# A hybrid layer on one core: one opening block with a quarter of x, and the causal attention's constants made beside the first FFN's choice

## The chip, the cores and the metric

The kernel runs on one core of one Trainium2 chip. The metric is the device time of one execution in microseconds (us), the median of several executions. A core has TensorE (PE), VectorE (DVE), ScalarE (ACT), GpSimd (POOL) and SyncE (SP). They run their own instruction streams and meet only at semaphores. In this kernel SP and ACT issue the DMAs. The kernel is a sequence of blocks; a block ends when every engine has come to its end, and the next one starts then.

## The reference, cut to what matters

x is 8 x 1024 tokens of 256 values, float32. Four sublayers are added to it one after the other, each on a layer norm of x:

```
x = x + attn_a(layernorm(x))     # 16 heads of 16; a query sees the keys at 40 offsets back (0..32, 48, 64, ... 384),
                                 # scores + pos_bias[offset, head], softmax; times sigmoid(x @ Wgate + bgate), @ Wout + bout
x = x + ffn(layernorm(x))        # 32 experts, each takes its 8 best tokens of a batch, merged by weight;
                                 # one row per expert through w1, gelu, w2; scattered back by weight
x = x + attn_b(layernorm(x))     # causal attention, 16 heads of 16, W1/b1 (q, k, v interleaved by head), W2/b2
x = x + ffn(layernorm(x))        # the same experts again
```

layernorm has no scale or shift: (x - mean) / sqrt(var + 1e-5).

## The kernel before

**The whole.** x stays in SBUF for the whole kernel as `x_sb`, 64 tiles of 128 tokens. The stages are: `build_constants` (L83), `band_attention` (L250), `ffn` "f1_" (L1480), `dense_attention` (L1007), `ffn` "f2_". Every sublayer leaves `bn_stats` of its new x in `stats`; the next one aggregates them to mean and variance (`bn_aggr`), ACT takes a square root (L364, L1104, L1537), DVE a reciprocal (L123), and `z` is the normalised x (L733, L1364, L1679).

**The opening.** `build_constants` is a block of its own: SP loads x in four quarters (L93), DVE runs `bn_stats` on each as it lands (L101), POOL builds the identity. Then comes the setup block of band attention (L317 to L407). SP loads weights and bias rows (L323 to L333), waits for DVE's `row_steps` and moves the split bias rows (L335). ACT loads the position biases (L351), waits until DVE has spread them over four short lines (L374 to L382), sends the lines to DRAM, each repeated for every row of a block (L355), waits until they have landed, and loads them back as sliding windows, `bias_k` and `bias_q`, with 12 DMAs (L362); then it takes the square root, and waits for the windows. DVE does the lines, a permutation, the normalizers of all 64 tiles (L393), the scaling of the q weights and the split of the bias rows into three bf16 parts (L403 to L406). In the block after it DVE first fills the ones rows of seven key stacks, three PSUM slots and `outT_ps` (L714 to L718), and POOL clears the value tiles (L464 to L466); PE and ACT wait for all of that (`cleared`).

**Band attention** follows a hand-written list of steps, `band_schedule()` (L149): each engine walks the same list and does its part of each step, so a step's place in the list is its place in every engine's and queue's order. A batch's heads come in four groups g of four. The steps: `z`, `zt` (PE transposes z, ACT copies), `q`/`k` (PE projects, DVE adds the bias), then its division into three bf16 parts for exactness (`part0` ACT, `rest1` POOL, `part1` ACT, `part2` POOL, each part stored to DRAM by ACT, the last as `store2`), `stack` (SP loads the parts back as stacked operands for two heads), `turn` (ACT and POOL reorder the stack for the far offsets, L870 and L502), `v`/`vout`/`vin` (values through DRAM), `mx` (PE scores for the row maxima, DVE reduces, L780), `fparts`, `fp`, `mred`, `mt`, `mrow` (the maxima of four heads become three bf16 rows under the queries' stack, by SP's DMAs L528), `S` (PE scores minus the maxima, DVE adds the position bias, L771, ACT exponentiates, L833), `PV`, `ote`, `ot`, `at`, `op`. PSUM gives three slots of two banks, used in turn by the steps that need one; a step waits until the slot's user three before it has been read. Projections of the next batch are put between the steps of this one (`fillers`, `between`), and the division of a q or k is spread over the steps behind it (L231 to L238). The first batch has no earlier one, so the list starts with its own opening (L204 to L207):

```
first = [("z", 0, 0), ("zt", 0, 0), ("z", 0, 1), ("zt", 0, 1)] + projection("q", 0, 0) + projection("k", 0, 0)
first += operands(0) + operands(1) + operands(2) + operands(3) + turned(0) + turned(1) + turned(2) + projection("q", 0, 1) + projection("k", 0, 1)
first += [step for i4 in range(2) for step in (("v", 0, i4), ("vout", 0, i4))]
first += [("mx", 0, 0, h) for h in range(HG)] + [("fparts", 0, 0), ("fp", 0, 0), ("mred", 0, 0), ("mt", 0, 0), ("mrow", 0, 0)]
```

**Causal attention** (`dense_schedule`, L915) is built in the same way, with SP storing and loading (`spill`, L1178, `stack`, L1190, `mrow`, L1195). `maxima(b, g)` gives 18 `mx` steps, then `mred`, `mt` and `mrow`; a stack holds four heads. The parts of q and k of a batch's first half (`projections(b, 0)`) feed stacks g = 0 and 1, those of the second half g = 2 and 3. Its list starts with L979 to L981:

```
seq = tokens(0) + projections(0, 0) + [("stack", 0, 0)] + projections(0, 1) + [("stack", 0, 1)] + values(0)
for steps in maxima(0, 0):
    seq += steps
```

Its setup block (L1068 to L1119) loads the weights with 13 DMAs of short runs on SP, builds a bf16 identity and the causal mask on POOL, and computes the normalizers and the parts of the bias rows on DVE. In the next block DVE fills the ones rows of three key stacks (L1350), `outT_ps` and `neg_off` before its first z.

**The FFN** has a setup block (L1521: normalizers, small loads, and the first 8 MB of expert weights into rings), a block that chooses the tokens (L1580: no work for SP and POOL in it; at its end DVE copies the merged tokens, L1739), and a block that runs the experts and adds the result to x (L1772).

## Time and profile before

| | |
|---|---|
| median of 3 runs | 3498.59 us (3488.94, 3498.59, 3508.78) |
| profiled execution | 3486.47 us, of which the span from first to last instruction is 3484.7 us |
| PE busy | 2844.4 us, 82% of the span |
| DVE busy | 1644.5 us, 47% |
| ACT busy | 1435.7 us, 41% |
| POOL busy | 794.2 us, 23% |
| mean granted TensorE clock | 0.914 of full speed |
| first matmul | 91.36 us |
| first instruction of f1_, of causal attention's setup | 1440.2 us, 1713.5 us |

Busy time is the time with an instruction of that engine in flight; the rest is waiting. "DVE ... [6.70 <-POOL b_parts L1217]" in a row of the timeline says that DVE was idle for 6.70 us before this instruction and that the last thing it waited for was POOL's instruction of line 1217 on `b_parts`. SPq and ACTq are the DMA issues of SP and ACT; their duration is that of issuing, not of the transfer. In the windows view the columns are the stretch, its length, the busy time (and instruction count) of PE, PE's weight loads, DVE, ACT and POOL, the granted TensorE clock, the share of the DMA engines and the GB/s that they moved.

### The profile page before, as it was taken

What the parts mean: (1) busy time and instruction counts of PE and PEld (TensorE: products, weight loads), DVE (VectorE), ACT (ScalarE), POOL (GpSimd) and SP (SyncE); (2) the same over time, 40 slices, a digit from 0 to 9 for tenths busy, and PEclk for the clock granted to TensorE, in tenths of its full rate; (3) what the DMA queues carried; (4) which work ended last, traced back from release to release, by engine and by line L of the source; (5) the groups of instructions that cost most, each with busy time, mean ns of one, the idle gap of its engine ahead of it and who ended that gap; (6) DMA issues with size and microseconds to landing.
All of it is one profiled execution on the core that took longest, in us unless ns stands there. A gap on an engine that the chain in (4) does not pass through costs nothing. (4 is left out here: it accounts for less than half of the span.)

```text
span 3484.7 us, 101224 instructions
## 1 busy us (share of the span) xinstructions
PE 2844.4 (82%) x45724; PEld 1622.0 (47%) x45724; DVE 1644.5 (47%) x2755; ACT 1435.7 (41%) x1422; POOL 794.2 (23%) x555
## 2 busy tenths in 40 slices
PE   0487888888888887689468989898989998997897
PEld 0255565655555555434234444444444444443443
DVE  5134434344344344520546666666665666664401
ACT  0245444444444453330115555454545454554401
POOL 0324343333434242000222112121211121210002
PEclk9778888889898989799669999999999999999998
DMA  5324233333324341259232212222222222220397
GB/s 142 86 57 113 73 84 79 92 88 78 94 63 106 78 99 48 106 230 403 62 91 50 61 43 60 46 57 50 59 49 56 55 56 56 56 47 35 158 422 265
DMA packets 233547, 344.23 MB, mean 99 GB/s; under 512 B 113690, under 2 KB 142180, under 8 KB 216740
## 3 DMA queue, kind: packets, MB, share of 16 engines
q1 hardware_dynamic: 207892, 310.02, 30.5%
q10 hardware_dynamic: 25232, 27.83, 3.5%
q8 instruction: 357, 5.85, 0.7%
q14 instruction: 66, 0.54, 0.1%
HBM read 266.15 MB, written 69.24 MB: 96 GB/s over the span
## 5 line engine op out<-in xcount | busy, mean ns | idle before, releaser
L1403 DVE TENSOR_REDUCE b_tops<-b_slot 128x8 f32<-128x1024 f32 x576 | 680.4, 1220 | 360.6 <-PE b_slot L1260 181.5
L1440 ACT ACTIVATE b_probs<-b_slot 128x1024 f32<-128x1024 f32 x576 | 582.5, 1022 | 549.6 <-PE b_slot L1260 393.2
L502 POOL COPY a_q_far<-a_q_near 96x1024 bf16<-96x1024 bf16 x128 | 259.1, 2054 | 344.9 <-PE a_slot L581 218.5
L1207 POOL TENSOR_SCALAR_AFFINE_SELECT b_probs<-b_probs 128x1024 f32<-128x1024 f32 x128 | 139.6, 1091 | 809.1 <-ACT b_probs L1440 809.1
L1280 PE MATMUL b_outT_ps<-b_probs,b_v 128*17 128x128 f32 (+3 forms) x4608 | 317.6, 383 | 6.2 <-ACT b_probs L1440 5.5
L1260 PE MATMUL b_slot<-b_q_stack,b_k_stack 99*128 99x512 bf16 (+3 forms) x1280 | 273.1, 320 | 43.8 <-DVE b_tops L1403 32.8
L870 ACT ACTIVATE a_k_far<-a_k_near 96x1024 bf16<-96x1024 bf16 x128 | 258.3, 2068 | 86.6 <-DMA a_k_near<-parts_near_dram 78.1
L1260 PE MATMUL b_slot<-b_k_stack,b_q_stack 96*128 96x512 bf16 (+3 forms) x1280 | 265.7, 322 | 29.5 <-DVE b_tops L1403 20.8
L771 DVE TENSOR_TENSOR a_probs<-a_slot,a_bias_k 128x1024 f32<-128x1024 f32 x128 | 154.6, 1218 | 192.4 <-PE a_slot L581 192.3
L780 DVE TENSOR_REDUCE a_tops<-a_slot 128x16 f32<-128x1024 f32 x128 | 156.3, 1222 | 118.1 <-PE a_slot L581 117.1
L833 ACT ACTIVATE a_probs<-a_probs 128x1024 f32<-128x1024 f32 x128 | 133.1, 1052 | 183.7 <-DVE a_probs L771 164.6
L1260 PEld LDWEIGHTS b_slot<-b_q_stack,b_k_stack 99*128 99x128 bf16 x1280 | 106.4, 99 | 203.7 <-DVE b_tops L1403 61.9
L1876 PE MATMUL f_ps<-f_w_ring,f_hidT 128*32 128x256 f32 x1024 | 184.0, 381 | 2.1 <-ACT f_hidT L1924 2.1
L1260 PEld LDWEIGHTS b_slot<-b_k_stack,b_q_stack 96*128 96x128 bf16 x1280 | 97.4, 98 | 185.0 <-DVE b_tops L1403 61.4
L621 PE MATMUL a_slot<-a_bias_q,a_ident 128*128 128x512 bf16 x256 | 102.3, 491 | 84.8 <-POOL a_q_far L502 27.0
L657 PE MATMUL a_outT_ps<-a_probs,a_v_near 128*17 128x64 f32 (+1 forms) x8448 | 152.8, 227 | 19.2 <-issue 15.3
L657 PEld LDWEIGHTS a_outT_ps<-a_probs,a_v_near 128*17 128x17 f32 x8448 | 127.9, 102 | 85.8 <-issue 76.8
L1855 PE MATMUL f_ps<-f_w_ring,f_lhs 128*32 128x512 f32 x512 | 146.7, 606 | 8.0 <-POOL f_lhs L1834 8.0
L1956 DVE TENSOR_TENSOR f_pre<-f_ps,f_b1T 128x128 f32<-128x128 f32 x32 | 7.8, 286 | 299.8 <-PE f_ps L1864 299.8
L1280 PEld LDWEIGHTS b_outT_ps<-b_probs,b_v 128*17 128x17 f32 x4608 | 96.3, 96 | 112.5 <-issue 68.1
L589 PE MATMUL a_slot<-a_zT,a_wqk 128*128 128x512 f32 x256 | 144.2, 670 | 3.9 <-issue 2.7
L799 DVE TENSOR_SCALAR a_zb<-a_slot,a_bqk 128x1024 f32<-128x1024 f32 x32 | 41.1, 1284 | 220.9 <-PE a_slot L589 180.6
(220 smaller groups left out, 4334.1 us busy)
## 6 DMA issues: line engine op xcount, KB each, us to landing
f_w_ring<-in_L_ffn_w_dram SPq DMA_DIRECT2D x128, 1024.0 KB, 9.1
parts_near_dram<-a_parts ACTq DMA_DIRECT2D x96, 256.0 KB
parts_dram<-b_parts SPq DMA_DIRECT2D x96, 256.0 KB
a_k_near<-parts_near_dram SPq DMA_DIRECT2D x128, 128.0 KB, 3.0
b_k_stack<-parts_dram SPq DMA_DIRECT2D x64, 256.0 KB, 6.9
a_q_near<-parts_near_dram SPq DMA_DIRECT2D x64, 192.0 KB, 2.9
b_q_stack<-parts_dram SPq DMA_DIRECT2D x32, 384.0 KB, 4.4
values_dram<-a_v_stage SPq DMA_DIRECT2D x16, 544.0 KB, 4.4
```

The source lines that it names most:

```text
L502: pool.tensor_copy(q_far[far][0:QK_ROWS, h, :].rearrange("p (r a) -> p r a", r=LINKS), q_near[near][0:QK_ROWS, h, :].rearrange("p (a r) -> ...
L589: return pe.matmul(dst[:, c * 512:(c + 1) * 512], wqk[:, "qk".index(kind), kd, 8 * part:8 * part + 8, :].rearrange("p h d -> p (h d)"), zT ...
L657: ins = pe.matmul(outT_ps[BLK * h:BLK * h + HD + 1, lo:top], v_near[:, c, blk % 4, (HD + 1) * h:(HD + 1) * (h + 1)], probs[h][:, at:at + t ...
L771: ins = dve.tensor_tensor(probs[h][:, :].rearrange("p (k t c) -> p k t c", k=2, c=64), src[:, :].rearrange("p (k t c) -> p k t c", k=2, c=64),
L780: ins = dve.tensor_reduce(tops[:, h, :, :].rearrange("p k t -> p (k t)"), src[:, :].rearrange("p (t c) -> p t c", c=64), AX.X, ALU.max)
L870: act.activation(k_far[far][0:QK_ROWS, h, :].rearrange("p (r a) -> p r a", r=LINKS), k_near[near][0:QK_ROWS, h, :].rearrange("p (a r) -> p ...
L1260: ins = pe.matmul(dst[:, at:at + top - lo], own[0:rows, head, P * tile:P * tile + P], other[0:rows, head, lo:top], start=True, stop=True)
L1280: ins = pe.matmul(outT_ps[32 * h:32 * h + HD + 1, first:last], v1[b % 2][:, j, HG * g + h, :], src[:, base + first:base + last], start=u = ...
L1403: ins = dve.tensor_reduce(out, src, AX.X, ALU.max)
L1440: act.activation(probs_of(b, g, u, h)[:, :], slot_of(step)[:, :], ACT.Exp).then_inc(taken_act, 1)
L1855: ins = pe.matmul(bank[n][32 * j:32 * j + 32, :], lhs1[half][:, kd, j, :], w1_ring[:, j, kd, n * 512:(n + 1) * 512], start=kd == 0, stop=k ...
L1876: ins = pe.matmul(bank[4 + half][32 * j:32 * j + 32, 0:D], hidT[half][:, c, j, :], w2_ring[:, j, c, :], start=c == 0, stop=c == HE // P - 1)
```

## The change

1. `build_constants` is gone. Its work is in band attention's setup block: SP issues one quarter of x first and the other three behind weights and rows; DVE runs `bn_stats` and the normalizers for this quarter (batches 0 and 1) alone; POOL builds both identities.
2. In that block POOL also does the memsets of the value tiles and of the seven key stacks' ones rows, and DVE those of the PSUM tiles. The semaphore `cleared` is gone. The windows (`bias_in`) are waited for by PE's first `mx` and DVE's first `S`, no longer by ACT at the block's end; ACT takes its square root behind the issue of the windows, as before.
3. The statistics of the other quarters are steps `x_stats` of the band's list (groups 0, 2 and 3 of batch 0), their normalizers the steps `norms` and `rstd` in group 0 of batch 1, with a square root on ACT.
4. Band attention's opening is reordered: v and the maxima of the first group come before the second half's q projection, whose k projection goes into the first group.
5. Causal attention's constants are allocated around the FFN and loaded and built in the FFN's choice block (SP, POOL, two scalings on DVE). Its setup block is gone; DVE computes the normalizers at the head of its main block. The memsets of the first stack, `outT_ps` and `neg_off` come behind the second z, those of the other two stacks ahead of DVE's copy of the first k.
6. Causal attention's opening is reordered: v first, then the second half's q and k between the first group's maxima, and stack (0, 1) behind them.

The diff, cut to its core:

```diff
-def build_constants(nc, ident, x, x_sb, stats):
...
 # band_schedule
             if not earlier:
-                return [], [], [("gate", b, 0)], [], [], [("gate", b, 1)]
+                return [], [("k", 0, 1)], [("gate", b, 0)], [("x_stats", 1, 0), ("x_stats", 1, 1)], [("x_stats", 1, 2), ("x_stats", 1, 3)], \
+                    [("gate", b, 1)]
...
-    first += operands(0) + operands(1) + operands(2) + operands(3) + turned(0) + turned(1) + turned(2) + projection("q", 0, 1) + projection("k", 0, 1)
+    first += operands(0) + operands(1) + operands(2) + operands(3) + turned(0) + turned(1)
     first += [step for i4 in range(2) for step in (("v", 0, i4), ("vout", 0, i4))]
-    first += [("mx", 0, 0, h) for h in range(HG)] + [("fparts", 0, 0), ("fp", 0, 0), ("mred", 0, 0), ("mt", 0, 0), ("mrow", 0, 0)]
+    first += [("mx", 0, 0, h) for h in range(HG)] + turned(2) + [("fparts", 0, 0)] + projection("q", 0, 1)
+    first += [("fp", 0, 0), ("mred", 0, 0), ("mt", 0, 0), ("mrow", 0, 0)]
...
+            if b == 0 and g in (2, 3):
+                place[3].extend([("x_stats", g, 0), ("x_stats", g, 1)])
+                place[4].extend([("x_stats", g, 2), ("x_stats", g, 3)])
+            if (b, g) == (1, 0):
+                place[4].append(("norms",))
+                place[5].append(("rstd",))
...
 # band_attention, setup block, SP
+                    quarter(0)
...
+                    for n in range(1, B // 2):
+                        quarter(n)
                     sp.wait_ge(row_steps, 6)
                     sp.dma_start(bias_rows[:, :, :], row_parts[0:1, :, :, :]).then_inc(rows_in, 16)
                     sp.wait_ge(weights_in, 16 * n_loads)
                     sp.wait_ge(rows_in, 64)
...
 # POOL
+                    pool.memset(v_near[:, :, :, :], 0.0)
+                    pool.memset(v_far[:, :, :], 0.0)
+                    pool.memset(v_stage[:, :, :, :], 1.0).then_inc(ident_made, 1)
+                    pool.wait_ge(ident_made, 5)
+                    for stack in k_near + k_far:
+                        pool.memset(stack[QK_ROWS:ALL_ROWS, :, :], 1.0)
...
 # ACT, behind the 12 DMAs of the windows
-                    act.wait_ge(stat_steps, STATS_STEPS)
-                    act.activation(std[:, :], std[:, :], ACT.Sqrt).then_inc(std_ready, 1)
-                    act.wait_ge(bias_in, 16 * 12)
+                    act.wait_ge(norm_steps, 2 * NT + 1)
+                    act.activation(std[:, 0:2 * NT], std[:, 0:2 * NT], ACT.Sqrt).then_inc(std_ready, 1)
...
 # DVE
+                    for slot in slots:
+                        dve.memset(slot[:, :], 0.0)
+                    dve.memset(outT_ps[:, :], 0.0)
...
-                    layer_norm_stats(dve, std_ready, stat_steps, stats, mv, std, rstd)
+                    dve.wait_ge(x_loaded[0], 16)
+                    for t in range(2 * NT):
+                        ins = dve.bn_stats(stats[:, t, :], x_sb[:, t, :])
+                    ins.then_inc(line_steps, 1)
+                    dve.wait_ge(line_steps, n_lines + 7)
+                    normalizers(dve, 0, 2 * NT, 0)
...
+                    dve.wait_ge(std_ready, 1)
+                    dve.reciprocal(rstd[:, 0:2 * NT], std[:, 0:2 * NT])
...
 # band_attention, main block, DVE
-                for stack in k_near + k_far:
-                    dve.memset(stack[QK_ROWS:ALL_ROWS, :, :], 1.0).then_inc(cleared, 1)
-                for slot in slots:
-                    dve.memset(slot[:, :], 0.0).then_inc(cleared, 1)
-                dve.memset(outT_ps[:, :], 0.0).then_inc(cleared, 1)
...
+                    elif kind == "x_stats":
+                        _, n, k = step
+                        dve.wait_ge(x_loaded[n], 16)
+                        for t in range(2 * n * NT + 4 * k, 2 * n * NT + 4 * k + 4):
+                            ins = dve.bn_stats(stats[:, t, :], x_sb[:, t, :])
...
 # dense_schedule
-    seq = tokens(0) + projections(0, 0) + [("stack", 0, 0)] + projections(0, 1) + [("stack", 0, 1)] + values(0)
-    for steps in maxima(0, 0):
-        seq += steps
+    seq = tokens(0) + projections(0, 0) + [("stack", 0, 0)] + values(0)
+    first, second = [step for steps in maxima(0, 0) for step in steps], projections(0, 1)
+    seq += first[:6] + second[:6] + first[6:12] + second[6:] + [("stack", 0, 1)] + first[12:]
...
 # dense_attention: the setup block (loads, identity, mask, parts of the bias rows, normalizers) is removed; main block, DVE
-                for n in range(DEPTH):
-                    dve.memset(k_stack[n][QK_ROWS:ALL_ROWS, :, :], 1.0).then_inc(cleared, 1)
-                dve.memset(outT_ps[:, :], 0.0).then_inc(cleared, 1)
-                dve.memset(neg_off[:, :, :], -LOWEST).then_inc(cleared, 1)
-                dve.wait_ge(cleared, N_CLEARED)
+                layer_norm_stats(dve, std_ready, stat_steps, stats, mv, std, rstd)
+                dve.wait_ge(stat_steps, STATS_STEPS + 1)
...
+                        if (b, i4) == (0, 1):
+                            dve.memset(k_stack[0][QK_ROWS:ALL_ROWS, :, :], 1.0).then_inc(cleared, 1)
+                            dve.memset(outT_ps[:, :], 0.0).then_inc(cleared, 1)
+                            dve.memset(neg_off[:, :, :], -LOWEST).then_inc(cleared, 1)
...
+                            if (kind, b, half) == ("k", 0, 0):
+                                for stack in k_stack[1:]:
+                                    dve.memset(stack[QK_ROWS:ALL_ROWS, :, :], 1.0).then_inc(cleared, 1)
...
 # ffn, choice block: SP issues the 13 loads (the two rows first) and the bias rows, POOL makes
 # identity, mask and the three parts of the rows (3 copies, 2 subtractions), DVE:
+                    if beside:
+                        dve.wait_ge(weights_in, 16 * n_loads)
+                        dve.tensor_scalar(dense["bqk"][:, 0, :], dense["bqk"][:, 0, :], HD ** -0.5, None, ALU.mult)
+                        dve.tensor_scalar(dense["wqk"][:, 0, :, :, :], dense["wqk"][:, 0, :, :, :], HD ** -0.5, None, ALU.mult)
                     dve.wait_ge(merge_done, B * NT)
...
 # build
-        build_constants(nc, ident, a["L0_attn_a_x"], x_sb, stats)
-        band_attention(nc, x_sb, stats, ident, attn_a, scratch)
-        ffn(nc, x_sb, stats, ident, experts, scratch, "f1_")
-        dense_attention(nc, x_sb, stats, ident, attn_b, scratch)
+        band_attention(nc, a["L0_attn_a_x"], x_sb, stats, ident, attn_a, scratch)
+        with ExitStack() as dense:
+            constants = dense_constants(nc, dense)
+            ffn(nc, x_sb, stats, ident, experts, scratch, "f1_", beside=(constants, attn_b))
+            dense_attention(nc, x_sb, stats, ident, constants, scratch)
```

## Rows read from the trace of the kernel before

**Rows 1.** Stretches (windows view): length, busy us of each engine, granted clock, DMA share, GB/s.

```profile
0.00:27.00 27.00, 0.00 (x0) 0.00 (x0) 15.97 (x48) 0.00 (x0) 0.70 (x6) 1.00 0.98 311
...
33.40:53.70 20.30, 0.00 (x0) 0.00 (x0) 8.64 (x123) 0.00 (x0) 0.60 (x3) 1.00 0.63 119
53.70:64.00 10.30, 0.00 (x0) 0.00 (x0) 0.92 (x4) 1.54 (x2) 0.00 (x0) 1.00 1.12 152
...
300.00:1400.00 1100.00, 918.90 (x27986) 636.23 (x27974) 463.76 (x632) 496.46 (x385) 388.14 (x244) 0.88 0.33 83
```

**Rows 2.** Timeline, setup: start us, length, engine, line, operation, out<-in, count [idle before].

```profile
0.82 14.46 SPq L93 DMA_DIRECT2D x_sb<-in_L_attn_a_x_dram  x4
...
9.19 5.32 DVE L101 BATCH_NORM_STATS2 stats<-x_sb 128x6 f32<-128x256 f32 x16 [9.19 <-DMA x_sb<-in_L_attn_a_x_dram]
...
33.38 0.41 ACTq L351 DMA_DIRECT2D a_pos<-n_L_attn_a_pos_bias_dram  x1
...
39.48 0.70 ACTq L355 DMA_DIRECT2D line_k_dram<-a_line_k  x1
...
53.69 1.94 ACTq L362 DMA_DIRECT2D a_bias_k<-line_k_dram  x4
...
62.79 0.26 ACT L364 ACTIVATE a_std<-a_std 128x64 f32<-128x64 f32 x1
...
67.90 0.85 SPq L335 DMA_DIRECT2D a_row_home<-a_row_parts  x1
70.35 1.91 POOL L464 MEMSET a_v_near<- 128x2176 f32 x1 [36.21 <-POOLq L317]
...
89.83 1.38 DVE L733 TENSOR_SCALAR a_zb<-x_sb,a_mv,a_rstd 128x256 f32<-128x256 f32 x4
```

**Rows 3.** Timeline, band attention, from its first projections to its first S.

```profile
97.86 16.30 PE L589 MATMUL a_slot<-a_zT,a_wqk 128*128 128x512 f32 x32 [1.11 <-ACT a_zT L877]
...
129.46 11.68 ACT L870 ACTIVATE a_k_far<-a_k_near 96x1024 bf16<-96x1024 bf16 x6 [11.91 <-DMA a_k_near<-parts_near_dram]
...
149.10 1.01 PE L621 MATMUL a_slot<-a_bias_q,a_ident 128*128 128x512 bf16 x2 [21.12 <-DVE a_zb L799]
...
161.96 1.02 ACT L881 ACTIVATE a_v_stage<-a_slot 128x1024 f32<-128x1024 f32 x1 [4.74 <-DMA values_dram<-a_v_stage]
...
167.49 1.22 DVE L780 TENSOR_REDUCE a_tops<-a_slot 128x16 f32<-128x1024 f32 x1 [0.91 <-PE a_slot L581]
...
179.47 0.61 PE L576 MATMUL a_slot<-a_q_near,a_k_near 99*32 99x64 bf16 x32 [5.28 <-DMA a_q_far<-a_row_home]
```

**Rows 4.** Timeline, end of the first FFN's choice: DVE takes the merged tokens.

```profile
1506.59 0.76 DVE L1739 COPY f_merged<-f_ps 128x256 f32<-128x256 f32 x2 [2.00 <-PE f_ps L1629]
```

**Rows 5.** Timeline, causal attention: setup block, memsets, first projections, first maxima, first S.

```profile
1713.51 4.32 DVE L117 BATCH_NORM_AGGREGATE b_mv<-stats 128x2 f32<-128x6 f32 x64 [0.30 <-PEq L1772]
...
1718.38 0.55 DVE L123 RECIPROCAL b_rstd<-b_std 128x64 f32<-128x64 f32 x1 [0.32 <-ACT b_std L1104]
...
1737.07 3.47 DVE L1350 MEMSET b_k_stack<- 3x4096 bf16 x1 [0.80 <-issue]
...
1746.13 1.38 DVE L1364 TENSOR_SCALAR b_zb<-x_sb,b_mv,b_rstd 128x256 f32<-128x256 f32 x4
...
1767.77 1.28 DVE L1409 TENSOR_SCALAR b_full<-b_slot,b_bqk 128x1024 f32<-128x1024 f32 x1 [6.70 <-POOL b_parts L1217]
...
1773.51 2.12 POOL L1217 TENSOR_TENSOR b_parts<-b_full,b_parts 128x1024 bf16<-128x1024 f32 x1 [1.17 <-ACT b_parts L1458]
...
1783.87 1.84 SPq L1190 DMA_DIRECT2D b_k_stack<-parts_dram  x4
...
1793.27 1.03 PE L1248 MATMUL b_slot<-b_later,b_ident 128*128 128x512 bf16 x2 [9.39 <-DMA b_k_stack<-parts_dram]
...
1798.61 18.19 DVE L1403 TENSOR_REDUCE b_tops<-b_slot 128x8 f32<-128x1024 f32 x16 [0.48 <-PE b_slot L1252]
...
1822.38 1.03 PE L1252 MATMUL b_slot<-b_q_stack,b_k_stack 99*128 99x128 bf16 x8 [3.40 <-DMA b_q_stack<-b_neg_rows]
```

398 lines of the change are left out of this document (194 added, 204 removed).

## The prediction

> **What bounds the kernel now.** I read first the busy shares of the page, then the stretches, then the timeline at the three places the diff touches. In the body of band attention PE is busy 919 of 1100 us at a granted clock of 0.88 [rows 1]: the body is PE's, and work put on DVE, POOL or a DMA queue there is cheap as long as PE does not wait. The places touched are different: there PE does nothing. The first z of band attention starts at 89.83 [rows 2], the first z of causal attention 32.6 us after its setup block starts [rows 5]. What ends these stretches is a chain through DMAs and DVE, and the change rebuilds both chains. All sums are against the profiled execution (3486.5 us, span 3484.7); it lies 12 us under the median of the three runs (3498.6), and I carry the difference of the sums over to that median.
>
> **1. The two opening blocks become one.** Before, x (four quarters, issued from 0.82) and its statistics come first, and everything else from 33.38 on. From there the chain is: ACT issues the position biases, DVE spreads them into lines, ACT sends the lines to DRAM at 39.48, waits 14.2 us, issues the windows from 53.69, and only then does the square root, ended at 63.05; DVE's bias rows go out at 67.90 and the block ends at 70.35. Then DVE's memsets hold z until 89.83 [rows 2].
> Removed: the 32.6 us (33.38 less 0.82) and the 19.5 us of memsets. Seven of those move to POOL, which has nothing else there: its own run at 1.91 us for 2176 elements, so seven of 2048 are some 13 us, and with the 4 of its first three memsets it is done by about 20 [rows 2]; hidden by the chain on ACT. The four PSUM memsets stay on DVE, about 4.3 us; some 2 of them outlast the landing of the biases, so they cost 2. Of the statistics, only a quarter stays: 5.3 us on DVE behind x's first quarter, which landed at 9.19 [rows 2], hidden as well.
> So without any collision the square root ends at 0.82 + 29.7 + 2 = 32.5 and z starts at about 34: the lower bound. But now x's last three quarters are issued by SP behind the weights, while ACT's lines and windows go out. DMA work of before, as share times length: x 26.5, weights with lines 12.8, windows 11.5 us [rows 1], together 50.8. If nothing of it overlaps better than before, the last transfer lands at 51.6, and with 2.5 us from the bias rows' issue to the block's end (67.90 to 70.35) z starts at 54: the upper bound. The new wait that I think decides: SP issues the bias rows last, behind 6 MB of x, and the block ends only when they have landed. x competes with the lines all the way and with about half of the windows: 0.8 + 26.5 + 12.8 + 5 = 45, plus 2.5: **z at 47, 43 us earlier** (36 to 56).
> The Trainium skill (DMA: Bandwidth & Descriptors, Queues, rings and completion order) says that each DMA engine takes the descriptors of one ring in ring order and takes turns between rings. By that the small bias rows wait for all of x; no row of before has a small load behind large ones. By the lower bound alone the total would be 13 us less.
>
> **2. Band attention's first steps.** z to the k projection is unchanged. Before, two more projections (q and k of the second half) with their divisions ran ahead of the maxima, so the first mx waited until 149.10 and the last ended at 168.71; S followed at 179.47 [rows 3]. After: two turns instead of three from 129.46 (a copy is 1.95, so four end at 137.3), the v copy 1.0, then 4.7 of waiting for its store and the second v copy: 144.1. Two maxima left from there, about 2.2 us each on PE and one reduction of 1.2: last mx at 149.8, 19 earlier. Then the q projection stands between: eight matmuls at 0.51 [rows 3], 4.1, taken as 6.8 on a PE that has idled; its division 7.9 from DVE's start to POOL's end (1767.77 to 1775.63 for the same steps, rows of causal attention [rows 5]); ACT can copy the maxima's rows only behind it (1 us and two store issues), then the row DMAs and S, 4 to 5. S at about 169: 10.4 earlier. The k projection goes into the first group: 3.6 us on PE, and stack (0,2,0), on SP, now waits for its division, so its turn comes some 4 us later on ACT and POOL, which the rest of the group covers. **Net 7 us earlier** (0 to 12).
>
> **3. Statistics beside band attention.** 48 bn_stats at 0.33 (5.32 for 16 [rows 2]) are 16 us on DVE in three groups, 2.7 at a time; 48 aggregations at 0.068 (4.32 for 64 [rows 5]) are 3.2; ACT gets one more square root and two table loads. DVE is busy 464 of 1100 us there [rows 1]. What would be late next is the mx behind 2.7 us of statistics, and so the next group's row maxima. **2 us later** (0 to 6).
>
> **4. Beside the first FFN's choice.** 13 small loads on SP, idle there, behind the expert weights; POOL, idle too, makes identity, mask and bias parts. DVE gets 0.56 us and a wait ahead of the merged copy, where it idles 2.00 [rows 4]. The loads fitted into the 32.6 us of their block before (1713.51 to 1746.13 [rows 5], memsets included) and now have the whole choice. **Nothing** (to 1.5 late).
>
> **5. Causal attention.** The block goes; the aggregation to reciprocal stays, from 1713.51 to 1718.93. z starts right after instead of at 1746.13 [rows 5]: **27.1 earlier**. The memset of the first stack, 4.3 with its gap, fits between z and q. The other two, 8.5 us, stand before the k copy in a gap of 6.70 [rows 5]: +1.8. Part of a store no longer competes with the first stack: -1. Then the order: the second half's q and k are put between the maxima, after 6 and after 12 of 18. Before, the first mx stood at 1793.27, DVE was through at 1816.80, S started at 1822.38, 29.1 after the first mx [rows 5]. DVE gets two copies of 1.28 and waits about 1.2 for each: +5, the lower bound. SP is worse: the order puts spill k, then stack (0,1), ahead of the DMA that S waits for. From the first mx: DVE takes k at 20.6, the division ends 7.9 later at 28.5, spill issues 1.9, stack issues 3.1 (1.84 for four of seven [rows 5]): the row DMA is issued at 33.5. Landing as before (3.1 after issue) S is at 36.6, +7.5; landing behind the stack, which needed 7.6 us after its last issue (1785.71 to 1793.27 [rows 5]), at 41, +12. I take +10.5. **Net 15.8 earlier** (12 to 22).
>
> **Sum:** -43 - 7 + 2 + 0 - 15.8 = -64. Profiled execution about 3423, median about **3435**.
>
> **Rivals.**
> A. *No collision of the DMAs:* x slips into the gaps of the lines (share 0.63 before [rows 1]), z at 34. For it: those gaps. Against: the windows ran at 1.12, without gaps. Total 13 less, 3422.
> B. *The DMA work adds up whole:* every transfer of the opening is paid on the same engines, the bias rows come last, z at 54. For it: x at 0.98 and the windows at 1.12 [rows 1] leave little to fill. 7 more, 3442. The Trainium skill (the same page, Issuing engines are not separate DMA queues) says this of the change: issuing from two engines saves only the time to issue. By rule and rows alike the gain of the merge is then 36.
> C. *The new orders are dear:* q's division keeps S of band attention where it was (+7), causal attention's S is 13 late (+2.5), the statistics cost 6 (+4): 3448; with PE at half speed in the added projections, 3455.
> D. *Slower:* granted clock of band attention. PE is the bound there, 919 us of 1100 at 0.88 [rows 1], a mean of stretches at 2.4 GHz and some at 1.2. No row here separates what PE did before it fell; if idling is what lowers it, and the new waits (late stack, rows behind stack, 2.7 us of statistics ahead of an mx) recur in each group, more is run at 1.2. Slower than before by 17.5 needs 81 us lost; of some 1050 us of PE work in this stage (0.84 of the 1260 from 180 to the FFN) that is 7.7%: 0.88 to 0.81. Against: most of the new waits occur once. At 0.80 the total would be 3530.
> E. *It does not do what it says:* lines and windows starve behind x until z is back at 80, and the new orders take back what causal attention's block gave. Then about 3489.
>
> **How the numbers follow.** Forecast 0.52, A 0.18, B 0.14, C 0.10, D 0.03, E 0.03. About 0.5% (17.5 us) is what a measurement of this kernel can tell from no change. Faster: forecast, A, B and C, 0.94; same: E, 0.03; slower: D, 0.03. The range: with every part at its late end the gains sum to 36 + 0 - 6 - 1.5 + 12 = 40.5, with every part at its early end to 56 + 12 + 22 = 90, so 3409 to 3458; the three runs lay some 10 us to either side of their median, so a few us are added at each end. 3405 to 3460 leaves out about 2 in 10.
>
> **What would show it.** Right: PE's first matmul at about 48; the last wait of the opening block on SP for the bias rows, with the DMA share near 1 until then; S of band attention about 79 us after z (89.6 before); POOL's memsets through by 20; no idle in the choice block at its DVE copy beyond 2; causal attention's z 5.5 us after the FFN; its S 86 to 87 us after z (76.3 before), its PE waiting there for the row DMA. Wrong: z above 54; PE's granted clock in band attention under 0.86; an mx waiting for DVE in groups 2 and 3 by more than 2 us.

## The result

The changed kernel takes 3451.85 us in the median (four runs, 3438.86 to 3457.64), the kernel before 3493.77 us in the runs beside it: a ratio of 0.9871, 95% interval 0.9822 to 0.992. A second measurement (changed_again, below) gave 0.9864 (0.9842 to 0.9886). So it is faster, by 42 us in the medians and 45 by the ratio. The forecast was 3435, 64 us faster; the range, 3405 to 3460, holds the result. The forecast is 17 us too low all the same: the sum of causal attention's terms was wrong by 18 us, and of the other terms some erred one way and some the other.

The profiled execution has a span of 3455.9 us (3484.7 before), with PE busy 2849.6 us and a mean granted clock of 0.915. To see where the time went I split each profile at nine starts: the first z, the first S, DVE's row copies of groups 8 and 31 of band attention, the first FFN (F1), DVE's copy of the merged tokens in it, causal attention's first z and first S, and the second FFN (F2). Groups are counted from 0. All profiles are in one table (us; differences of start times in the timelines; "before" is the profile of the rows ahead of the prediction):

```
profile             z     z-S   S-g8  g8-g31 g31-F1 F1-merged merged-z z-S   S-F2   F2-end span
before              89.8  89.6  304.8 900.3  55.7   66.3      239.5    76.2  1388.6 273.7  3484.7
before_again        89.9  90.5  302.6 902.3  56.2   66.3      240.1    76.6  1389.8 272.9  3487.3
before_third        89.9  89.8  305.9 903.2  57.3   67.8      239.3    76.7  1394.1 272.5  3496.6
the changed kernel  44.5  74.8  312.3 913.7  56.1   69.6      214.5    103.6 1394.0 272.8  3455.9
changed_again       43.8  77.4  314.5 904.7  56.7   68.9      214.0    104.3 1390.0 274.3  3448.6
band_order_before   43.7  90.0  311.5 912.8  56.8   68.2      214.7    102.3 1391.5 274.0  3465.5
x_late              36.6  76.2  321.4 909.1  56.4   69.9      213.5    103.5 1389.4 272.1  3448.0
stats_open          48.4  77.7  306.1 903.4  56.6   68.8      214.7    104.0 1387.9 273.7  3441.2
stats_gap           43.7  75.2  321.1 906.9  56.6   68.9      214.6    101.8 1393.0 273.8  3455.7
stack_late          43.8  76.4  306.7 909.8  55.2   66.3      214.5    91.6  1404.3 272.7  3441.4
rows_dve            43.8  74.4  312.1 903.8  55.8   67.5      213.0    104.5 1391.3 271.8  3438.1
dense_order_before  43.9  76.2  309.7 915.5  57.0   69.0      214.9    80.1  1395.0 273.6  3435.1
order_memset        43.9  76.2  313.2 906.4  55.4   67.3      214.0    76.5  1393.8 273.8  3420.4
all_mends           37.0  77.2  327.0 903.3  54.7   66.8      213.6    77.0  1392.2 273.0  3421.9
```

The mean of the two profiles of the changed kernel against that of the three before: z 45.7 earlier, z to S of band attention 13.9 shorter, S to group 8 9.0 longer, groups 8 to 31 7.3 longer, the choice to the merged copy 2.5 longer, from there to causal attention's z 25.4 shorter, its z to S **27.5 longer**, the rest 1.7 longer. That is 37, the difference of the mean spans (3489.5 and 3452.3).

Single profiles scatter. Six of them have the same instructions in band attention (the changed kernel twice, stack_late, rows_dve, dense_order_before, order_memset): their S to group 8 lies at 306.7 to 314.5 us, mean 311.4, and groups 8 to 31 at 903.8 to 915.5. A difference of a few us in these two columns between single profiles says little.

### The profile page after: what moved, and what is told of

It reads as the page before. It is cut to its first block and busy times, and to the rows that moved or that the text cites. A ratio compares the mean times of both kernels' runs of the same rounds, so it can differ in the third digit from the quotient of the medians.

```text
span 3455.9 us, 101201 instructions
## 1 busy us (share of the span) xinstructions
PE 2849.6 (82%) x45724; PEld 1626.4 (47%) x45724; DVE 1634.9 (47%) x2745; ACT 1438.2 (42%) x1425; POOL 809.4 (23%) x567
## 5 line engine op out<-in xcount | busy, mean ns | idle before, releaser
L1238 PEld LDWEIGHTS b_outT_ps<-b_probs,b_v 128*17 128x17 f32 x4608 | 96.4, 96 | 112.5 <-issue 68.5
L1170 POOL TENSOR_TENSOR b_full<-b_full,b_parts 128x1024 f32<-128x1024 f32 x32 | 68.1, 2129 | 336.2 <-ACT b_parts L1418 336.2
```

What stands on the lines that cost most here:

```text
L1238: ins = pe.matmul(outT_ps[32 * h:32 * h + HD + 1, first:last], v1[b % 2][:, j, HG * g + h, :], src[:, base + first:base + last], start=u = ...
```

## The profile after, place by place

**The opening.** Timeline of the changed kernel, setup block (start, length, engine, line, operation, out<-in, count, idle before), which answers to [rows 2]:

```profile
10.78 13.33 SPq L338 DMA_DIRECT2D x_sb<-in_L_attn_a_x_dram  x3
...
12.01 0.70 ACTq L387 DMA_DIRECT2D line_k_dram<-a_line_k  x1
...
14.10 3.80 ACTq L387 DMA_DIRECT2D line_q_dram<-a_line_q  x1
24.16 3.95 SPq L359 DMA_DIRECT2D a_row_home<-a_row_parts  x1
29.54 1.97 ACTq L394 DMA_DIRECT2D a_bias_k<-line_k_dram  x4
31.54 7.20 ACTq L394 DMA_DIRECT2D a_bias_q<-line_q_dram  x4
...
40.16 2.24 ACTq L394 DMA_DIRECT2D a_bias_q<-line_q_dram  x2
...
43.97 0.25 DVE L449 RECIPROCAL a_rstd<-a_std 128x16 f32<-128x16 f32 x1 [20.31 <-ACT a_std L396]
```

```profile
0.00:27.00 27.00, 0.00 (x0) 0.00 (x0) 19.75 (x103) 0.00 (x0) 17.31 (x19) 1.00 0.99 307
27.00:44.50 17.50, 0.00 (x0) 0.00 (x0) 0.25 (x1) 1.50 (x2) 0.00 (x0) 1.00 1.17 231
```

z came at 44.53; 47 was forecast. The DMA share is at 1 nearly to the end, as forecast. But the last wait is DVE's for ACT's square root, not SP's for the bias rows: z starts 0.31 us after the reciprocal. SP had issued the bias rows by 28.1. ACT's own chain had grown: lines to windows 17.5 us (14.2 in [rows 2]), and four windows whose issue alone took 7.20 us. Both engines lost time in issuing: three quarters of x 13.33 us, one small line 3.80.

**Causal attention's opening.** Timeline of the changed kernel from the memsets to the first S, which answers to [rows 5]:

```profile
1704.12 3.47 DVE L1369 MEMSET b_k_stack<- 3x4096 bf16 x1 [3.02 <-PE b_slot L1256]
1708.39 3.47 DVE L1369 MEMSET b_k_stack<- 3x4096 bf16 x1 [0.80 <-issue]
1711.90 1.28 DVE L1372 TENSOR_SCALAR b_full<-b_slot,b_bqk 128x1024 f32<-128x1024 f32 x1
...
1737.59 1.01 PE L1206 MATMUL b_slot<-b_later,b_ident 128*128 128x512 bf16 x2 [24.41 <-DMA b_k_stack<-parts_dram]
...
1761.35 1.28 DVE L1372 TENSOR_SCALAR b_full<-b_slot,b_bqk 128x1024 f32<-128x1024 f32 x1 [4.16 <-PE b_slot L1256]
...
1767.08 2.12 POOL L1175 TENSOR_TENSOR b_parts<-b_full,b_parts 128x1024 bf16<-128x1024 f32 x1 [1.17 <-ACT b_parts L1422]
1769.23 1.88 SPq L1136 DMA_DIRECT2D parts_dram<-b_parts  x3
...
1771.21 2.99 SPq L1148 DMA_DIRECT2D b_q_stack<-parts_dram  x3
...
1771.70 0.22 DVE L1377 COPY b_neg_rows<-b_slot 96x128 bf16<-96x128 bf16 x1 [0.43 <-PE b_slot L1275]
1774.24 2.02 SPq L1148 DMA_DIRECT2D b_k_stack<-parts_dram  x4
1776.31 0.81 SPq L1153 DMA_DIRECT2D b_q_stack<-b_neg_rows  x1
...
1789.09 1.03 PE L1210 MATMUL b_slot<-b_q_stack,b_k_stack 99*128 99x128 bf16 x8 [17.43 <-DMA b_q_stack<-b_neg_rows]
```

z itself started 5.5 us after the stage before, as forecast (32.6 before). The memsets were meant for the 6.70 us gap ahead of the k copy; they stand behind the wait for PE's k projection, so the k copy is at z + 26.45, 4.8 later than before. The row copy is done at 1771.92, but SP issues its DMA 4.4 us later, behind the stack, and S starts 12.8 us after that issue (3.1 before). One row tells what is lost besides: PE waits **24.41 us** for the first stack before its first maximum (9.39 in [rows 5]). In the old order the second half's projections stood in that wait.

## The experiments

Every time below is the median of the runs with its ratio to the kernel before on the same chip; stretches are from the table.

### 1. Causal attention's old order alone

```diff
-    seq = tokens(0) + projections(0, 0) + [("stack", 0, 0)] + values(0)
...
-    seq += first[:6] + second[:6] + first[6:12] + second[6:] + [("stack", 0, 1)] + first[12:]
+    seq = tokens(0) + projections(0, 0) + [("stack", 0, 0)] + projections(0, 1) + [("stack", 0, 1)] + values(0)
+    for steps in maxima(0, 0):
+        seq += steps
```

> The changed kernel with only causal attention's opening order put back: both halves of q and k and both stacks ahead of the values and of the 18 maxima. In the changed kernel S of causal attention started 103.64 us after its z (76.25 before the change). Theory: the interleaved order costs this (two projections on a cold PE and their copies between the maxima, then the second stack and the row DMA behind it): S starts 29 us after the first mx again, 81 to 83 after z, and the total falls by 20 to 25 us against the changed kernel's 3452. Rival 1: the late S comes from the constants and weights made beside the FFN's choice or from the memsets of the stacks: S stays at 100 or more after z, total within 5. Rival 2: S comes 20 earlier, but the first groups lose it again, because stack (0,1) and the values stand behind one another in other places: total within 5 of 3452.

Measured: 3418.82 us, 0.9794 (0.975 to 0.9838). z to S fell from 103.6 and 104.3 to 80.1, DVE's first reduction stayed at z + 52.8 (54.0 and 53.6), and S stands 27.3 us behind it (27.2 before the change). The first rival (constants beside the choice are late) falls. So does the second (the first groups lose it again): S to the second FFN is 3 us longer than the mean of the two, within the scatter of that stretch (1387.9 to 1395.0 in all profiles but stack_late). The new order brought the first mx hardly any gain and cost some 23 us.

### 2. The second stack behind the row DMA

```diff
-    seq += first[:6] + second[:6] + first[6:12] + second[6:] + [("stack", 0, 1)] + first[12:]
+    seq += first[:6] + second[:6] + first[6:12] + second[6:] + first[12:] + [("stack", 0, 1)]
```

> The changed kernel with stack (0,1) issued behind the row DMA that S waits for, instead of ahead of it. Theory of the prediction: S waits because the row DMA is issued behind that stack's seven issues and lands behind its 1.5 MB; then the row DMA is issued at the row copy's end, 4.4 us earlier, and lands 3 to 4 us later instead of 12.8: S 12 to 14 us earlier, 90 to 92 after z, total 10 us or more lower. Rival, which I hold likelier: the first mx of the next group stands on PE right behind the first S and needs that very stack; S comes 12 to 14 earlier and PE then waits for the stack, which lands at about the same time as before: total lower by less than 4, and the chain that costs is the late second k projection, its division, its spill and the stack.

Measured: 3450.52 us, 0.9895 (0.9851 to 0.9939). Timeline around the first S:

```profile
1757.87 0.81 SPq L1153 DMA_DIRECT2D b_q_stack<-b_neg_rows  x1
1758.79 2.12 SPq L1148 DMA_DIRECT2D b_q_stack<-parts_dram  x3
1760.95 2.11 SPq L1148 DMA_DIRECT2D b_k_stack<-parts_dram  x4
...
1764.42 1.04 PE L1210 MATMUL b_slot<-b_q_stack,b_k_stack 99*128 99x128 bf16 x8 [6.84 <-DMA b_q_stack<-b_neg_rows]
...
1773.97 1.03 PE L1206 MATMUL b_slot<-b_later,b_ident 128*128 128x512 bf16 x2 [8.51 <-DMA b_k_stack<-parts_dram]
```

S came 12 to 13 us earlier (91.6), and PE then waited 8.51 us for the stack. S to the second FFN grew by 12 (1404.3, against 1392.0 in the changed kernel). The total is that of the changed kernel. So the row DMA's place, on which the prediction put its price, is the name of the last wait and not its cause. The cause is the chain behind it: second k projection, division, spill, stack, which the next group's first maximum needs right behind the first S.

### 3. The old order with the memsets elsewhere

The memsets of stacks 1 and 2 move from ahead of the first k copy to ahead of the first maximum's reduction; the order is that of experiment 1.

```diff
                         src = slot_of(step)
+                        if step == ("mx", 0, 0, 0, 0):
+                            for stack in k_stack[1:]:
+                                dve.memset(stack[QK_ROWS:ALL_ROWS, :, :], 1.0).then_inc(cleared, 1)
                         dve.wait_ge(filled, nth["filled", step])
...
-                            if (kind, b, half) == ("k", 0, 0):
-                                for stack in k_stack[1:]:
-                                    dve.memset(stack[QK_ROWS:ALL_ROWS, :, :], 1.0).then_inc(cleared, 1)
```

> The changed kernel with causal attention's opening order put back and the memsets of stacks 1 and 2 moved from ahead of the first k copy to ahead of the first maximum. They stood behind the wait for PE's k projection, not in the gap ahead of it, and the k copy came 26.5 us after z (21.6 before the change). Theory: k copy at 21.6 to 22.5 after z, first mx at 47 to 49, S at 75 to 76.5 after z (80.1 with the order alone), total 4 to 5 lower than with the order alone. Rival: DVE then does them ahead of the first maximum and that waits for them: S at 79 to 84.

Measured: 3418.12 us, 0.9785 (0.9769 to 0.9802), the fastest of all, though not to be told from experiment 1 by its total. The stretch is clear: z to S 76.5, as before the change; DVE's first reduction at z + 49.4, 3.4 earlier than in experiment 1. Timeline:

```profile
1713.84 1.28 DVE L1371 TENSOR_SCALAR b_full<-b_slot,b_bqk 128x1024 f32<-128x1024 f32 x1 [6.69 <-POOL b_parts L1174]
1716.03 3.47 DVE L1357 MEMSET b_k_stack<- 3x4096 bf16 x1 [0.91 <-issue]
1720.30 3.47 DVE L1357 MEMSET b_k_stack<- 3x4096 bf16 x1 [0.80 <-issue]
...
1723.83 1.04 PE L1205 MATMUL b_slot<-b_later,b_ident 128*128 128x512 bf16 x2 [9.82 <-DVE b_k_stack L1357]
```

The rival holds in part: PE's first maximum now waits for the second of these memsets.

### 4. Band attention's old opening order

```diff
-                return [], [("k", 0, 1)], [("gate", b, 0)], [("x_stats", 1, 0), ("x_stats", 1, 1)], [("x_stats", 1, 2), ("x_stats", 1, 3)], \
+                return [], [], [("gate", b, 0)], [("x_stats", 1, 0), ("x_stats", 1, 1)], [("x_stats", 1, 2), ("x_stats", 1, 3)], \
...
-    first += operands(0) + operands(1) + operands(2) + operands(3) + turned(0) + turned(1)
+    first += operands(0) + operands(1) + operands(2) + operands(3) + turned(0) + turned(1) + turned(2) + projection("q", 0, 1) + projection("k", 0, 1)
...
-    first += [("mx", 0, 0, h) for h in range(HG)] + turned(2) + [("fparts", 0, 0)] + projection("q", 0, 1)
-    first += [("fp", 0, 0), ("mred", 0, 0), ("mt", 0, 0), ("mrow", 0, 0)]
+    first += [("mx", 0, 0, h) for h in range(HG)]
+    first += [("fparts", 0, 0), ("fp", 0, 0), ("mred", 0, 0), ("mt", 0, 0), ("mrow", 0, 0)]
```

> The changed kernel with only band attention's opening order put back: turn 2 and the second half's q and k projections ahead of the maxima. In the changed kernel S started 74.8 us after z (89.6 before the change), but by group 2 the lead over the kernel before had fallen by 8.8 us, after a wait for stack (0,2,0). Theory: S is again 89 to 90 after z, the wait for that stack is gone, group 2 stands 5 to 7 us later than in the changed kernel, total 5 to 7 higher. Rival 1: the whole 14.9 is worth keeping and the loss to group 2 has other causes (statistics, clock): total 12 to 15 higher. Rival 2: the order is worth nothing: within 3.

Measured: 3458.45 us, 0.9904 (0.9876 to 0.9932). z to S is 90.0. From z to the row copy of group 8 it takes 401.5 us, against 387.1 and 391.9 with the new order (383.1 to 391.9 in the six profiles, mean 387.3): the order is worth 12 to 14 us, and the ratios of the totals differ by 12 to 14 us too. That is rival 1's size, not the theory's 5 to 7. The late stack (0,2,0) is real in the changed kernel (timeline, first group; ACT's turn waits for it):

```profile
123.65 6.17 PE L595 MATMUL a_slot<-a_zT,a_wqk 128*128 128x512 f32 x8
...
144.71 3.34 SPq L530 DMA_DIRECT2D a_k_near<-parts_near_dram  x4
151.21 4.03 ACT L888 ACTIVATE a_k_far<-a_k_near 96x1024 bf16<-96x1024 bf16 x2 [11.33 <-DMA a_k_near<-parts_near_dram]
```

The 8.8 us that the theory set against the order are real against the kernel before, but no loss of the order: from DVE's first row copy to its second it takes 43.5 us in the changed kernel, 34.7 before and 35.5 here, and that stretch now holds the second half's k projection, which stood ahead of S before.

### 5. x out of the opening block

SP issues quarter n at the end of group n - 1 of band attention; the statistics of quarter 1 move to group 1.

```diff
-                    for n in range(1, B // 2):
-                        quarter(n)
...
-            if b == 0 and g in (2, 3):
+            if b == 0 and g in (1, 2, 3):
...
+            if b == 0 and g < 3:
+                seq.append(("x_in", g + 1))
```

> The changed kernel with the last three quarters of x (6 MB) taken out of the opening block and loaded at the ends of groups 0, 1 and 2 of band attention; their statistics stand in groups 1, 2 and 3. In the changed kernel z started at 44.5; the windows were issued 17.5 us after the lines (14.2 before the change) and ACT was held 7.2 us in issuing four of them (2.1 before). Theory: x in the same DMA engines caused both, and ACT's chain ends the block: lines to windows 14 us, the four issues 2 us, the square root 8 to 10 us earlier, z at 34 to 37, total 6 to 10 us lower. Rival 1: SP's bias rows behind x end the block together with ACT: the same z, but the last wait of the block in the changed kernel was not ACT's. Rival 2: ACT is slow for another reason (issue of 8 windows in the rows' form): z stays at 43 or more. Rival 3: z is early, but 6 MB among the stacks of groups 0 to 2 costs as much: total within 3.

Measured: 3449.59 us, 0.9891 (0.9846 to 0.9936). Timeline of its setup block:

```profile
26.69 1.95 ACTq L394 DMA_DIRECT2D a_bias_k<-line_k_dram  x4
28.67 2.13 ACTq L394 DMA_DIRECT2D a_bias_q<-line_q_dram  x4
...
36.00 0.25 DVE L449 RECIPROCAL a_rstd<-a_std 128x16 f32<-128x16 f32 x1 [12.36 <-ACT a_std L396]
36.57 1.06 DVE L739 TENSOR_SCALAR a_zb<-x_sb,a_mv,a_rstd 128x256 f32<-128x256 f32 x3 [0.31 <-PEq L336]
```

The same four windows are issued in 2.13 us instead of 7.20, lines to windows is 14.7, z is at 36.57. So x in the DMA engines delayed ACT's chain by 8 us, part of it in the issue. It is no gain: S to group 8 takes 321.4 us instead of 313.4. Rival 3 holds beside the theory, in two ways that the waits of that stretch show (x_late from 225 to 270 us, then the changed kernel from 236 to 275; line waited for, us, times, longest):

```profile
DVE stats L762 <- DMA x_sb<-in_L_attn_a_x_dram: 4.5, 1, 4.5
ACT a_k_far L892 <- DMA a_k_near<-parts_near_dram: 9.8, 2, 9.4
```

```profile
ACT a_k_far L888 <- DMA a_k_near<-parts_near_dram: 4.4, 1, 4.4
```

The last quarter of x lands too late for its own statistics, and ACT waits 5 us longer for a stack. The stretch from the fourth row copy to the fifth takes 39.0 us here and 42.1 in all_mends, the two kernels with x moved; in all others with the change it is 32.0 to 34.9.

### 6 and 7. The statistics, in the opening block and in DVE's gap

In stats_open DVE does all 64 statistics and aggregations in the opening block, behind the bias rows, and ACT one square root:

```diff
-                    normalizers(dve, 0, 2 * NT, 0)
...
+                    for n in range(1, B // 2):
+                        dve.wait_ge(x_loaded[n], 16)
+                        for t in range(2 * n * NT, 2 * (n + 1) * NT):
+                            ins = dve.bn_stats(stats[:, t, :], x_sb[:, t, :])
...
+                    normalizers(dve, 0, B * NT, 0)
```

In stats_gap they stay beside band attention, at the ends of groups 1 to 3, with the normalizers at the end of group 4:

```diff
-                place[3].extend([("x_stats", g, 0), ("x_stats", g, 1)])
-                place[4].extend([("x_stats", g, 2), ("x_stats", g, 3)])
+                place[5].extend([("x_stats", g, k) for k in range(4)])
```

> The changed kernel with the statistics, aggregations and the square root of all 64 tiles back in the opening block, behind the bias rows on DVE; x is loaded where the change has it. In band attention there are none. Theory: the statistics beside band attention cost 3 us in group 3 (PE waited 3.4 us for the row maxima, 0.5 before) and 2 to 4 in group 5 (the 48 aggregations), while in the opening block they are nearly hidden, since x has landed by 35 and ACT's windows hold z until 44 anyway: z at 44 to 48, group 3 at 39.5 to 40 us and group 5 at 37 to 38.5 again, total 2 to 6 lower. Rival 1: the two groups' extra time is clock scatter or the new orders: they stay at 42.6 and 40, and the total is 0 to 4 higher for the later z. Rival 2: DVE's work delays the bias rows and z to 52 or more: total higher by 3 or more.

> The changed kernel with the statistics of each later quarter of x moved, whole (5.3 us), to the end of groups 1, 2 and 3, behind the row copy, where DVE idles 8.8 us in each group; aggregation and reciprocal stand at the end of group 0 of the second pair. Theory: what costs is not DVE's time but its place ahead of the last maximum and the row maxima: at the end of a group it is hidden. From the first S to the row copy of group 8: 303 to 308 us (312 to 316 with the change, 306 with the statistics in the opening block), groups 3 and 5 at 39.5 to 40.5 and 36.5 to 39, z still at 44; total 4 to 8 lower than the changed kernel's 3450. Rival: DVE's load as such, or clock scatter, costs: 311 or more, total within 3.

Measured: stats_open 3446.82 us, 0.9882 (0.9863 to 0.9902); stats_gap 3448.34 us, 0.9862 (0.9832 to 0.9893). PE's waits in group 3 (from the third row copy to the fourth; line waited for, us, times, longest), first the row maxima's in the kernel before, then the changed kernel, then stats_open:

```profile
PE a_slot L640 <- DVE a_neg_parts L751: 0.5, 1, 0.5
```

```profile
PE a_slot L629 <- ACT a_k_far L888: 5.9, 1, 5.9
PE a_slot L648 <- DVE a_neg_parts L753: 3.4, 1, 3.4
```

```profile
PE a_slot L627 <- POOL a_q_far L510: 5.1, 1, 5.1
...
PE a_slot L646 <- DVE a_neg_parts L751: 0.4, 1, 0.4
```

Without statistics group 3 takes 39.9 us (42.6 with them, 39.5 before) and group 5 37.4 (40.1; 36.8). In the six profiles with the changed kernel's band attention the means are 42.5 and 40.4, so the statistics cost some 5.6 us in these two groups. S to group 8 is 306.1, which is 7.3 less than in the two profiles of the changed kernel and 5.3 less than the mean of the six: 5 to 7 us, not 2. The later z (48.4) takes 4 of them back, which is why the total hardly moves. stats_gap does not hide them either. Timeline of DVE at the end of group 2 there:

```profile
204.18 1.28 DVE L813 TENSOR_SCALAR a_zb<-a_slot,a_bqk 128x1024 f32<-128x1024 f32 x1 [8.81 <-PE a_slot L592]
205.38 5.31 DVE L755 BATCH_NORM_STATS2 stats<-x_sb 128x6 f32<-128x256 f32 x16
210.60 1.20 DVE L785 TENSOR_TENSOR a_probs<-a_slot,a_bias_k 128x1024 f32<-128x1024 f32 x1
```

The gap of 8.81 us is there, but ahead of a projection's copy, and the statistics stand behind that copy, in front of the next S. My theory fell there; it is the memsets' mistake again. How much that costs one profile can't say. S to group 8 is 321.1, 8 more than in the changed kernel, but the four stretches that hold statistics or normalizers are only 3.5 us longer than the mean of the six (163.5 and 160.0). Most of the 8 stand in a group without any, from the seventh row copy to the eighth (windows view, stats_gap, then the changed kernel):

```profile
357.60:405.90 48.30, 37.64 (x1003) 23.50 (x989) 17.75 (x27) 19.14 (x15) 19.05 (x12) 0.79 0.36 93
```

```profile
354.20:396.80 42.60, 33.63 (x1003) 21.87 (x989) 17.76 (x27) 19.12 (x15) 19.32 (x12) 0.84 0.41 105
```

The instructions are the same and the granted clock is lower, 0.79 against 0.84; why, no run tells. The total is that of the changed kernel.

### 8. The bias rows split by DVE

```diff
-                        pool.wait_ge(rows_in, 32)
-                        for part in range(PARTS):
-                            pool.tensor_copy(row_parts[:, part, :, :], row[:, :, :]).then_inc(row_steps, 1)
...
+                        dve.wait_ge(rows_in, 32)
+                        dve.wait_ge(row_steps, 4)
+                        for part in range(PARTS):
+                            dve.tensor_copy(row_parts[:, part, :, :], row[:, :, :]).then_inc(row_steps, 1)
...
```

> The changed kernel with the bias rows of causal attention split by DVE at the end of the choice block (five operations on one partition) instead of by POOL in its middle. With the change four of DVE's z operations took 3.5 to 3.9 us instead of 1.38 while POOL split the rows, and the merged copy came 69 us after the block's start (66.3 before). Theory: POOL's operations slow DVE down, and through it PE and the choice: here the four take 1.4 us, the merged copy is at 66 to 67, since DVE's own five operations (about 2 us) lie where it idles or just ahead of the copy (then up to 68), total 1 to 3 lower. Rival 1: the small loads behind the expert weights slow DVE: the four still take 3.5. Rival 2: the rows land so late that DVE waits for them: merged copy at 70 or more.

Measured: 3441.48 us, 0.9854 (0.9824 to 0.9884). Timeline of the choice block in the changed kernel, then in this one (the same four z operations):

```profile
1411.59 17.76 SPq L1565 DMA_DIRECT2D b_wqk<-in_L_attn_b_W_dram  x2
...
1429.87 0.60 POOL L1591 CAST f_row_parts<-f_row 1x512 bf16<-1x512 f32 x1 [18.00 <-DMA f_row<-in_L_attn_b_b_dram]
1430.24 3.49 DVE L1695 TENSOR_SCALAR f_zb<-x_sb,f_mv,f_rstd 128x256 f32<-128x256 f32 x4
1430.55 1.14 POOL L1594 TENSOR_TENSOR f_row<-f_row,f_row_parts 1x512 f32<-1x512 f32 x1
```

```profile
1418.98 1.38 DVE L1688 TENSOR_SCALAR f_zb<-x_sb,f_mv,f_rstd 128x256 f32<-128x256 f32 x4
```

DVE's part stands just ahead of its merged copy. The theory holds for the four operations: together 1.38 us without POOL's rows beside them, in this kernel and in all_mends; with the loads alone, no slowing. The merged copy is 67.5 us after the block's start (66.8 in all_mends; nine profiles with POOL's rows: 66.3 to 69.9, mean 68.5; three of the kernel before: mean 66.8), so the gain is 1 to 2 us, at the edge of what single profiles can tell. That the four operations are what delays the merged copy is argued, not shown.

### 9. All of it together

> The changed kernel with all that the runs pointed to: x's later quarters at the ends of groups 0 to 2, their statistics at the ends of groups 1 to 3, causal attention's opening order of before, the memsets of stacks 1 and 2 ahead of the first maximum, and the bias rows split by DVE. If the gains add up (8 for z, 5 to 7 for the statistics, 27 for causal attention's S with 4 of it kept by the memsets, up to 3 for the rows): 3400 to 3410. Rival: x among the stacks of groups 0 to 2 takes back its 8 (with x alone moved, the first S to group 8 took 321 us against 312): 3410 to 3418, no better than the order and the memsets alone.

The edits of experiments 3, 5 and 8 and stats_gap's (its statistics in place of those of experiment 5), in one kernel. Measured: 3420.07 us, 0.9781 (0.9755 to 0.9808), with z at 37.0 and z to S of causal attention 77.0, but S to group 8 at 327.0. The rival holds: with x and the statistics moved, z is 7 us earlier and S to group 8 16 us longer than the mean of the six. It is no better than experiment 3, which needs two edits alone and beats both kernels: 30 us faster than the changed one by the medians, 74 to 75 faster than the one before.

### 10 to 12. The kernels again, and the stage in between

> The changed kernel once more, unaltered. After the first S of band attention it took 1282 us to the first FFN, against 1261 before the change, and the four variants run so far took 1272 to 1287. Of this the opening groups explain some 10. Theory 1: the rest is scatter of the granted clock from run to run (single executions of one kernel lay up to 20 us apart): here that stage lies anywhere from 1270 to 1287, and a second execution of the kernel before is as far off its first. Theory 2: the change makes the whole stage slower: both executions at 1280 or more. The opening stretches repeat within 1.5 us: z at 43.5 to 45, S 75 to 76.5 after it; causal attention's S 102 to 104 after its z.

> The kernel before the change once more, unaltered, for a second profile. From the row copy of group 8 to that of group 31 of band attention the two kernels issue the same instructions apart from nothing; it took 900 us in the first profile and 909 to 916 in five profiles with the change. Theory 1 (clock scatter): this one takes 905 to 915. Theory 2 (the change slows that stretch through where its buffers lie or what runs beside): 900 to 902 again.

> The kernel before the change, unaltered, for a third profile. Groups 8 to 31 of band attention, whose instructions the change leaves alone, took 900.4 and 902.3 us before it, and 903 to 916 (mean 909) in eight profiles with it. If the granted clock only scatters: 905 or more here. If the kernel before has more of it there: 899 to 904 again.

Measured: changed_again 3448.5 us; the profiled executions of before_again 3489.01 and before_third 3498.37. From the first S to the first FFN changed_again took 1275.9 us (1282.1 in the first profile of the changed kernel, 1260.8 before), so not both are at 1280 or more, as theory 2 asked, and neither is near the time before. From the row copy of group 8 to that of group 31 both kernels do the same work (the same instruction counts, PE some 22,840 each), and the three profiles before lie at 900.3, 902.3 and 903.2 us, the eleven with the change or a variant at 903.3 to 915.5, mean 908.1. The granted clock there is 0.88 to 0.90 before and 0.87 to 0.89 after, a mean of stretches at 2.4 GHz and some at 1.2. So theory 1, scatter alone, does not explain it well: some 6 us more with the change, in a scatter of 12, and every one of the eleven is above all three of before. **This stays open.** No run tells a cause.

## Why the prediction was right or wrong

**1. Setup (-43; measured -45.7).** The size was right, the named wait was not. The step said that the block ends with the bias rows, behind 6 MB of x. It ended with ACT's chain, 8 us late through the same x, by experiment 5. x_late's z (36.6) is nearly rival A's (34), and what it gained was lost elsewhere. SP's load of x does hold ACT's DMAs up. The Trainium skill (DMA: Bandwidth & Descriptors, Queues, rings and completion order) has each DMA engine take one ring's descriptors in order. By that rule small loads wait for large ones of the same queue, and the trace agrees: causal attention's bias line, issued by SP behind the 8 MB of expert weights, was there for POOL 18.00 us into its wait.

**2. Band opening (-7; measured -12 to -14).** The first S came 13.9 us nearer to z (10.4 forecast), and of what followed only 2 were given back (3.4 reckoned). Rival C's "q's division keeps S where it was" is refuted by experiment 4.

**3. Statistics (+2; measured +5 to +7).** The right mechanism with the wrong size: the wait of PE for the row maxima grew from 0.5 to 3.4 us in group 3, which is a sign that the prediction had named as one of being wrong. Group 5 lost as much where the 48 aggregations stand, which the step had priced as DVE time and not placed. The range ended at 6, so the size lies at its edge or past it.

**4. Choice (0, to 1.5 late; measured +2.5 in two profiles, +1.7 in the mean of nine).** The step counted POOL as idle and asked only whether the loads fit. It did not ask what POOL does to DVE. Four z operations took 3.49 us together (1.38 elsewhere) beside POOL's one-partition operations, and probably through them the merged copy came later. The Trainium skill (SBUF — State Buffer, Who interferes with whom) says that DVE in its two-port modes and GpSimd exclude each other for whole instructions; whether these four ran in such a mode no run shows, but the trace agrees in so far as DVE was held up beside POOL, by 2.1 us here.

**5. Causal attention (-15.8; measured +2).** This is the step that failed. -27.1 for the block was right (z 5.5 us after the FFN), though the FFN's last stage gave back 2 of it. The memsets' +1.8 was 4.8, since the gap lay ahead of a wait that they stand behind. The order's +10.5 was 22.4. By its own sum: DVE takes k 23.8 us after PE's first mx (20.6 forecast; PE's projections took 3.7 and 6.2 us instead of 3.6), the division 7.9 (as forecast), the spill 1.9, the stack's issue 5.1 (3.1), the landing 12.8 (3.1 to 7.6). Beyond the sizes the frame was wrong: the step priced the added work on DVE and SP only, and did not see that in [rows 5] this work already stood in PE's wait for the first stack. Moving it out lengthened that wait (9.39 to 24.41 us) and brought the first mx no earlier. Experiment 1 returns 24 us of the lost 27.5, experiment 3 the rest.

**The total.** That it lies in the range is partly luck. The causal term was to bring 12 to 22 us and cost 2, outside its own bounds, and groups 8 to 31 took 7 us more that no term had; the band's opening and z, 5 to 7 and 3 us better than forecast, and the ends of the range, which added up all other parts at their latest, made room for that.

**The forecast against the rivals.** B (3442) and C (3448) came nearer to the total than the forecast, but by sums that did not happen: z was not at 54, and S of band attention was not late. D's mechanism did not show: the clock in groups 8 to 31 was 0.87 to 0.89 in all profiles with the change, far from 0.81, even if some 6 us there are unexplained. (D's last figure is off by its own terms: 1050 us of work at 0.88 take 105 us more at 0.80, so 3540 and not 3530.) E did not happen. The gain from causal attention's block, 25 us after the merged copy, was given back whole, 27.5 us, by the new order and the two memsets in the next 104 us.

## What to carry to other kernels

Before a step is moved out of a stretch, look whether it stands in a wait for a DMA there: then it was free, and its new place is not. "There is a gap of 6.7 us ahead of this copy" holds only for work issued ahead of the wait; behind it, the gap is gone. Two memsets of 8.5 us in all, placed so, cost 4.8 us instead of 1.8, and three sets of statistics gained nothing by their move. Before a difference of a few us is given a cause, look how far single profiles of the same instructions lie apart: here up to 8 us in 310. And when the last wait is for a small DMA behind a large one, check who else needs the large one before the small one is moved ahead.

## What the runs showed of the hardware that I had not expected

- Issuing is not constant in cost. Four window DMAs took ACT 7.20 us to issue with 6 MB of x under way and 2.13 us without (experiment 5); two loads of short runs behind 8 MB of weights held SP for 17.76 us (1.75 us for the same two in their own block of the kernel before).
- POOL's copies and subtractions on one partition (0.60 and 1.14 us each) stretched four DVE operations from 1.38 to 3.49 us in all; with the rows on DVE they took 1.38 (experiment 8).
- A row DMA of SP took 3.1 us from issue to use before, 12.8 us behind a stack of seven DMAs, and 6.6 us behind a spill of three (experiment 2).

The two loads in their own block before (timeline of the kernel before, where the issue takes 1.75 us):

```profile
1713.46 1.75 SPq L1074 DMA_DIRECT2D b_wqk<-in_L_attn_b_W_dram  x2
```
